# A block of windowed attention and mixed experts on one core: expert weights from another DMA queue, and another order in the tail

## What is computed

```
h = layernorm(x) * (1 + ca) + sa
x = x + ga * attention(h)
h = layernorm(x) * (1 + cb) + sb
x = x + gb * experts(h)

attention: q, k, v = h @ wq, wk, wv              16 heads of 8 channels
  local  = softmax over a causal window of 32, on k and v
  remote = softmax over 64 pooled latents (8 heads), then @ r_out_w
  out    = (sigmoid(q . gl) * local + sigmoid(q . gr) * remote) @ w_out

experts: g   = mean over tokens of (relu(h @ gate_w1.T + gate_b1) @ gate_w2.T + gate_b2)   one of 8 per expert and batch
  mW1 = W1 + sum over e of g[e] * TW1[e]         F = 512 rows of 128
  mW2 = W2 + sum over e of g[e] * TW2[e]         128 rows of 512
  out = gelu(h @ mW1.T + mb1) @ mW2.T + mb2      biases mixed likewise
```

## Time and profile before

| | us |
|---|---|
| three runs | 706.54, 707.58, 707.37; median 707.37 |
| profiled execution, its own time | 706.55 |
| its span in the trace | 704.7 |
| busy in the span: PE / PE weight loads / DVE / ACT / POOL | 662.0 / 503.2 / 542.8 / 382.1 / 217.1 |
| chain that ended last, shares | PE 78%, DVE 16%, issue 3%, ACT 1% |
| DMA: SP's queue (q1) / POOL's queue (q0) | 18.25 MB, 10.7% / 6.31 MB, 5.8% of the 16 engines |

### The profile page before, as it was taken

How to read it: one execution, slowest core, us unless ns; L and a number is a source line. 1 busy time by engine, 2 the same in 40 slices (tenths; PEclk the granted TensorE clock), 3 DMA queues, 4 the chain that set the end, 5 groups by cost and what they waited for, 6 DMA issues and landing times.

```text
span 704.7 us, 24615 instructions
## 1 busy us (share of the span) xinstructions
PE 662.0 (94%) x9075; PEld 503.2 (71%) x9075; DVE 542.8 (77%) x1242; ACT 382.1 (54%) x907; POOL 217.1 (31%) x351
## 2 busy tenths in 40 slices
PE   4698999999999999999999999999869999999998
PEld 2365676667766667776667666677559899998996
DVE  5777898999998999999999989998757255472552
ACT  2264666567766577765677665677522423324232
POOL 3344444344533345443345443454320000000000
PEclk9799999999999999999999999999979999999999
DMA  4656410110011110101100101100500110000001
GB/s 108 170 79 87 57 31 22 30 30 22 22 30 24 34 24 22 30 22 28 32 22 22 30 22 30 30 15 16 74 3 2 30 32 7 30 22 30 30 8 52
DMA packets 65797, 24.84 MB, mean 35 GB/s; under 512 B 38440, under 2 KB 64360, under 8 KB 65648
## 3 DMA queue, kind: packets, MB, share of 16 engines
q1 hardware_dynamic: 64320, 18.25, 10.7%
q0 software_dynamic: 1456, 6.31, 5.8%
HBM read 16.13 MB, written 8.40 MB: 35 GB/s over the span
## 4 chain that ended last, share of the span: by engine, by line
PE 78%; DVE 16%; issue 3%; ACT 1%; DMA 0%; POOL 0%; DVEq 0%; SPq 0%; POOLq 0%
PE SB L822 8%; PE WB L810 8%; PE SB L889 7%; DVE rden L639 7%; PE WB L975 7%; PE WB L921 5%; PE WB L940 5%; PE WB L797 4%; PE WB L925 4%; PE SB L797 4%; DVE mx L553 3%; DVE Pr L560 3%; PE SB L1036 3%; PE WB L849 3%; PE WB L837 3%
## 5 line engine op out<-in xcount | busy, mean ns | idle before, releaser
L390 ACT ACTIVATE Pr<-Pr 128x512 f32<-128x512 f32 x128 | 77.8, 638 | 130.8 <-DVE Pr L560 130.6
L498 ACT ACTIVATE Pr<-WB,mb1T 128x256 f32<-128x256 f32 x128 | 49.8, 477 | 75.7 <-PE WB L810 75.6
L560 DVE TENSOR_TENSOR Pr<-SB,mx 128x512 f32<-128x512 f32 x128 | 84.9, 684 | 3.6
L553 DVE TENSOR_REDUCE mx<-SB 128x8 f32<-128x512 f32 x128 | 84.6, 682 | 3.8 <-PE SB L874 3.8
L364 POOL TENSOR_TENSOR attT<-a_gated,rem_g 128x256 f32<-128x256 f32 x32 | 23.2, 724 | 172.7 <-DVE a_gated L654 172.7
L395 ACT COPY PT<-SB 128x512 f32<-128x512 f32 x128 | 75.1, 589 | 2.1 <-PE SB L889 2.1
L639 DVE RECIPROCAL rden<-WB 128x256 f32<-128x256 f32 x32 | 56.2, 1758 | 22.0 <-PE WB L925 22.0
L335 POOL TENSOR_TENSOR KM<-K_ch,bd_scale 128x1024 f32<-128x1024 f32 x32 | 60.6, 1894 | 37.9 <-ACT K_ch L407 37.9
L889 PE MATMUL SB<-ident,Pr 128*128 128x128 f32 x512 | 66.8, 273 | 1.1 <-ACT Pr L390 1.0
L975 PE MATMUL WB<-GKBD,GQT 128*128 128x512 f32 (+1 forms) x128 | 56.4, 524 | 7.0 <-DVE wait_carrier L740 4.9
L889 PEld LDWEIGHTS SB<-ident,Pr 128*128 128x128 f32 x512 | 58.8, 141 | 5.1 <-ACT Pr L390 1.4
(11 more groups left out here) (188 smaller groups left out, 1419.7 us busy)
## 6 DMA issues: line engine op xcount, KB each, us to landing
x_all<-in_L_attn_x SPq DMA_DIRECT2D x32, 128.0 KB, 2.1
v_rows<-V_rows SPq DMA_DIRECT2D x32, 128.0 KB, 1.8
VBD<-v_rows SPq DMA_DIRECT2D x128, 32.0 KB, 1.8
TW<-in_L_ffn_TW POOLq DMA_DIRECT2D x16, 256.0 KB, 10.0
GA<-ga_rows POOLq DMA_DIRECT2D x1, 2048.0 KB, 11.8
out_x<-attT SPq DMA_DIRECT2D x16, 128.0 KB, 1.8
out_x<-y_ga SPq DMA_DIRECT2D x16, 128.0 KB, 1.8
PT<-in_L_ffn_W SPq DMA_DIRECT2D x2, 256.0 KB
```

Of the source, the lines that this page charges most:

```text
L390: nc.scalar.activation(Pr[:, k, :], Pr[:, k, :], ACT.Exp).then_inc(p_ready, 1)
L553: nc.vector.tensor_reduce(mx[:, k, :], SB[k][:].rearrange("p (h j) -> p h j", h=8), AX.X, ALU.max).then_inc(mx_ready, 1)
L560: nc.vector.tensor_tensor(Pr[:, k, :].rearrange("p (w h c) -> p h w c", w=2, h=8), SB[k][:].rearrange("p (h w c) -> p h w c", w=2, h=8), b ...
```

## The change

Three things change. First, `load_experts` moves from POOL to SP: SP writes out its steps 3 to 10 and issues expert it - 3 at the end of each, behind VBD, so two DMAs of 256 KB a step; its loop covers 11 to 30. POOL's `after` keeps only the load of GA. Second, `experts(0, 1, 0)` moves on DVE and PE from behind step B + 1 to behind step B + 2; on PE it stands in front of the waits and mixes that were there. Third, DVE's steps B + 2 and on no longer put y_ga first: it stands at the usual place, in step B + 2 behind the statistics of batch 30.

```diff
@@ -278,13 +278,22 @@
                         sp.dma_start(VBD[W * h:W * h + W, :, h, :], v_dram[:, h, :].rearrange("(k c) n -> c k n", c=W)
                                      ).then_inc(vbd_loaded, 16)
 
+            def load_experts(e):
+                sp.dma_start(TW1[J * e:J * e + J], ins["L0_ffn_TW1"][e].rearrange("(i j) h -> j i h", j=J)
+                               ).then_inc(tw_loaded, 16)
+                sp.dma_start(TW2[J * e:J * e + J], ins["L0_ffn_TW2"][e].rearrange("(i j) f -> j i f", j=J)
+                               ).then_inc(tw_loaded, 16)
+
             step(0)
             sp.wait_ge(zeros_ready, 1)
             load(rest_w, w_loaded)
 
             step(1)
             step(2)
-            with sp.Fori(3, B - 1) as it:
+            for it in range(3, 3 + E):
+                step(it)
+                load_experts(it - 3)
+            with sp.Fori(3 + E, B - 1) as it:
                 step(it)
             step(B - 1)
             step(B)
@@ -313,12 +322,6 @@
             nc.gpsimd.affine_select(out=tri[:], in_=tri[:], compare_op=ALU.is_ge, fill=0.0, base=0,
                                     pattern=[[-1, P]], channel_multiplier=1).then_inc(mask_ready, 1)
             nc.gpsimd.memset(VBD[:], 0.0).then_inc(pv_done, 1)
-
-            def load_experts(e):
-                pool.dma_start(TW1[J * e:J * e + J], ins["L0_ffn_TW1"][e].rearrange("(i j) h -> j i h", j=J)
-                               ).then_inc(tw_loaded, 16)
-                pool.dma_start(TW2[J * e:J * e + J], ins["L0_ffn_TW2"][e].rearrange("(i j) f -> j i f", j=J)
-                               ).then_inc(tw_loaded, 16)
 
             def inv_std(b, aggr, mv, ve, eps, rstd, rstd_s):
 
@@ -372,9 +375,6 @@
                     pool.dma_start(ga_dram, ga_row).then_inc(ga_stored, 16)
                     pool.wait_ge(ga_stored, 16)
                     pool.dma_start(GA[:], bc(ga_dram.rearrange("b d -> (b d)"), [P, B * D], 0)).then_inc(ga_loaded, 16)
-                if 1 <= it < 4 or it == B:
-                    for e in range(2 * (it - 1), 2 * it) if it < 4 else range(6, E):
-                        load_experts(e)
 
             pipeline(pool, step, after)
 
@@ -585,9 +585,6 @@
                                         bc(GA[:, bass.ds(b * D, D)], [P, T, D], 1), ALU.mult).then_inc(yga_ready, 1)
 
             def step(it):
-                tail = isinstance(it, int) and it >= B + 2
-                if tail and has(it, 3):
-                    output_times_ga(it - 3)
                 if has(it, 4):
                     dve.wait_ge(x1_ready, it - 4 + 1)
                     stats(x_all[:, bass.ds((it - 4) * S, S)], st_d, stat_d, mv_d, aggr_d, it - 4)
@@ -613,7 +610,7 @@
                 if has(it, 1):
                     latent_lowered(it - 1, *latent_tiles[0])
                     latent_maximum(it - 1, 1, NL)
-                if has(it, 3) and not tail:
+                if has(it, 3):
                     output_times_ga(it - 3)
                 if has(it, 1):
                     latent_lowered(it - 1, *latent_tiles[1])
@@ -695,7 +692,7 @@
                 nc.vector.tensor_tensor(gmb2T[:, cols], mb2T[:, cols], gbT[:, cols], ALU.mult).then_inc(g_ready, 1)
 
             def after(it):
-                if it == B + 1:
+                if it == B + 2:
                     experts(0, 1, 0)
                 if it == B + 3:
                     for m in range(8):
@@ -1054,9 +1051,8 @@
                 mm(biases[:, FC * n_b:(FC + 1) * n_b], tb2[:], gT[:, cols], start=True, stop=True).then_inc(g_done, 1)
 
             def after(it):
-                if it == B + 1:
+                if it == B + 2:
                     experts(0, 1, 0)
-                if it == B + 2:
 
                     pe.wait_ge(tw_loaded, N_TW)
                     pe.wait_ge(g_ready, N_G0)
```

## The result

The changed kernel takes 703.76 us, the median of five runs (701.43 to 704.37), beside 707.37 us for the kernel before on the same chip. The ratio is 0.9945 with an interval of 0.9926 to 0.9964: 0.55% faster. The forecast was 703.2 us. The profiled execution took 703.73 us, its span is 701.8 us against 704.7 us.

The account below looks back on a forecast made before the run. It took PE's chain of waits as the bound, with 5.5 us lost in steps 3 and 4 beside POOL's loads. Front -5.5 plus tail +1.3 gave -4.2: 703.2 us from the median 707.37; range 701.2 to 706.8.

Parts of the forecast that it names:

- The front: Steps 3 and 4: waits, stops and low clock go, 2.09 + 2.14 + 1.32 = 5.55, taken as 5.5 us gained.
- Parts 1 and 2: Steps 3 and 4: PE's waits before the latent scores go (2.09 us), and stops inside the scores go (2.14 us).
- first rival: Stops inside the scores come from code length alone and stay, with the low clock; 706.6 us, chance 12%.
- part 2: Steps 3 and 4: instruction fetches no longer meet expert loads, so both stops inside the scores go, 2.14 us.
- Part 3: Step 3's gates (L951) through the next first projection run at full clock without the idle stretches: 1.32 us gained.
- SP's load: Two more DMAs on SP in each of eight steps fit into its 8.6 us gap and cost 0.
- room of 17.7 us: Time SP's added loads may take before costing: gap 8.6, wait for values 2.7, slack before V_rows copy 6.4 us.
- part 4: SP's added issues (0.9 us a step) and 512 KB transfers (some 5 us) fit its gap, costing 0.
- The tail: After the last attT: projection and statistics come earlier, but gates at low clock stand before the mixes; 1.3 us lost.
- from there the order is that of before: Tail after batch 31's transposes, forecast at 526.1 against 524.76: same order as before, so the loss stays 1.3 us.
- mild rival: The tail costs nothing: clock stays up or returns sooner, gates take 1.7 us; 701.9 us, chance 16%.

Follow-up runs that it names:

- loads alone: Kernel before with the expert loads moved to SP as in the change, tail as before; 701.99 us, ratio 0.9926.
- burst from SP: Kernel before with SP issuing the expert loads at POOL's old moments (behind steps 1, 2, 3 and 32), tail as before; 712.18 us, ratio 1.0068.
- POOL paced: Changed kernel's tail, but POOL issues the loads, one expert in each of steps 3 to 10, its steps 0 to 10 written out; 710.29 us, ratio 1.0043.
- 1 MB a step: Changed kernel with two more unused 256 KB loads behind each expert on SP; 706.05 us, ratio 0.9973.
- 2 MB a step: Changed kernel with six more unused 256 KB loads behind each expert on SP; 760.65 us, ratio 1.0748.
- tail-only: Kernel before with the tail of the change, loads still on POOL; 708.65 us, ratio 1.0013.
- order-only: Kernel before with only DVE's tail order changed, statistics of batch 30 ahead of the last y_ga; 706.84 us, ratio 0.9992.
- gates-only: Kernel before with only the first gates moved behind step B + 2; 711.15 us, ratio 1.0056.
- the fillers: Unused products in PE's idle time: changed kernel, one place, 702.44 us; kernel with gates taken apart and spread earlier, three places, 695.45 us.

## Why the prediction was right

**The front, 5.5 us forecast.** The loads alone bring 5.2 us by the ratio. In the pair of profiles it is 4.82, and 4.68 + 1.28 = 5.96 for steps 3 and 4 alone; what lies between is the long step 2, in which PE does the same work in both and the clock stays low for longer. Step 3 was forecast at 14.3 us and took 13.79, step 4 at 15.6 and took 15.68.

*Parts 1 and 2* came true in the result, but they are not two gains that stand side by side. The run with the burst on SP shows that the time of POOL's issues (1.68 us in step 3) was hidden behind the late fetch: with the issues gone and the burst left, the whole 3.35 us became one stop. Only the sum of 4.23 us could be had, and only by moving the burst. The first rival, which was to keep the stops and still win 2.09, was priced wrongly for the same reason, and so was the expectation of 705 us for that run. That the stops are the loads' doing is shown by this table, read from the DMA view in narrow stretches and from the timelines of PE. "Burst" is the time from the first packet of the expert loads to the last (or of the unused loads beside them), "fetch" the packets of q8.

| kernel, place | burst | fetch, us it took | PE goes on at | stopped for |
|---|---|---|---|---|
| before, step 3 | 50.0 to 60.4 | 59.95, 1.15 | 62.50 | 1.67 |
| before, step 4 | 67.5 to 77.0 | 76.84, 1.21 | 79.41 | 0.47 |
| burst from SP, step 3 | 50.6 to 59.9 | 61.17, 1.19 | 63.55 | 3.49 |
| burst from SP, step 4 | 68.2 to 77.6 | 78.40, 1.14 | 80.91 | 1.59 |
| burst from SP, tail | 501.4 to 511.0 | 510.27, 1.80 | 513.45 | 2.74 |
| POOL paced, step 3 | 54.3 to 59.2 | 58.29, 1.78 | 61.26 | 2.41 |
| POOL paced, step 4 | 72.0 to 76.3 | 75.64, 2.05 | 79.10 | 3.19 |
| 1 MB a step, step 4 | 60.6 to 69.4 | 69.37, 1.85 | 72.51 | 2.28 |
| 2 MB a step, step 4 | 59.5 to 78.4 | 78.65, 1.11 | 81.03 | 8.43 |
| changed, step 3 | none | 57.27, 0.96 | | 0 |
| changed, step 4 | 61.4 to 66.7 | 63.09, 1.91; 71.61, 0.88 | | 0 |
| loads alone, step 4 | 61.8 to 66.0 | 67.02, 1.20; 72.22, 1.29 | | 0 |

In all nine stops the fetch comes when the burst is nearly or just through, and PE goes on 1.2 to 1.4 us after the fetch has landed. The burst comes from either queue, with 0.5 to 2 MB, and the longest burst goes with the longest stop. Where a burst ended early in the step, PE did not stop, whether the step's first fetch came in it (changed) or just behind it (loads alone); the second one, which was late in the kernel before (76.84), then comes 5 us after the burst, as part 2 had it. The burst isn't the only thing that makes such a stop: the 1 MB kernel has one of 0.17 us in step 2, ahead of its first expert load, 1.4 us after a fetch that landed at 43.61. So a small part of a stop can be the code's own, as the first rival says.

The rule quoted in the prediction from the Trainium skill (DMA: Bandwidth & Descriptors, section Issuing engines are not separate DMA queues), that another issuer saves only the time of issuing, fits here: SP at POOL's moments brought no gain, but a loss of 4.8 us. What the change wins comes from the moment, not from the queue: expert 0 is issued at 60.3 us, after the fetch at 57.27.

*Part 3*, the clock: forecast 1.32 us for L951 and the projection behind it. In this pair of profiles they give 1.92 - 1.13 = 0.79 and 1.06 - 0.59 = 0.47 us, 1.26 in all. As a term of its own that was luck. In the tail-only, order-only and gates-only kernels, with the loads still on POOL and the stops of step 3 in place, the clock did not fall in step 3: the gates take 1.03 us there (in the gates-only kernel it fell in step 4 instead). Yet steps 3 and 4 together take 35.35, 35.08 and 36.26 us, against 35.43 in the kernel before, because PE then waits longer for GKBD in step 4, 1.66 to 1.67 us and not 0.41. So what the clock costs is for the most part time that PE would have waited anyway. The sum of 5.5 us is right, as what two steps lie above the steady one; how it splits into parts 1 and 3 changes from one profile to the next.

**SP's load, 0 forecast.** The verdict was right, the room of 17.7 us was not. That step of part 4 added up the slack in front of three waits, as for one late transfer. A load that comes back every step can't use slack twice: SP's own round has to fit into the step, so between the end of the VBD issue and the landing of the V_rows store there are 14.95 - 1.8 = 13.1 us. With 1 MB it takes 8.6 + 3.3 = 11.9 us, and the steps stay at 14.95 to 14.98 us. With 2 MB it takes 4.4 + 17.1 = 21.5 us, and the step becomes 23.3 us. By the 17.7 us that step should have cost 3.8 us, not 8.3.

**The tail, +1.3 us forecast.** By the ratios it is 0.9 us (tail alone), and 1.3 and 0.6 us (the two builds of the changed kernel against the loads alone); the intervals are about as wide as that. The forecast's path fits at nearly every link, counted from attT:

| | forecast | changed kernel |
|---|---|---|
| statistics of batch 30 | -0.1 | -0.16 |
| xn_d of batch 30 | 2.0 | 2.05 |
| its transposes | 3.0 | 2.99 |
| twelve small matmuls take | 3.0 | 2.73 |
| mixes | 10.1 | 9.82 |
| transposes of batch 31 | 13.2 | 13.37 |
| ffn1 against before | +1.3 | +1.96 |

The last line misses 0.7 us. The mixes begin 0.97 us late, and from them to `ffn1` it takes 10.28 us against 9.28: the first sixteen mix matmuls take 3.76 us against 3.20, the next sixteen 2.23 against 1.95. The clock comes back later in them than before, which "from there the order is that of before" left out. And the pair of profiles is not the whole case: with the very order of before, the loads-only kernel had its mixes at 9.65 and ffn1 at 19.77 us, only 0.3 us better than the change, since the clock fell 0.3 us into its small matmuls. Over all profiles `ffn1` comes 19.46 to 20.79 us behind attT with the new order (changed kernel twice, tail alone, POOL paced, 1 MB, 2 MB; 19.9 on average) and 18.14 to 19.77 us with the old one (before, loads alone, burst from SP; 19.1 on average). What the new order costs depends on when the clock falls, and the old order can pay nearly the same. That is why the times show less than 1.96 us, and that the forecast of 1.3 us fits is in part luck. The mild rival (clock up, tail free) needs idle times filled; the fillers show that the changed order doesn't get there by itself.

**Open.** How the chip orders a fetch among the packets of a burst isn't shown: the trace has no record of when PE asked, and in the 2 MB kernel one fetch came 1.7 us into the burst while the next had to wait for its end. A run in which POOL issues at exactly SP's moments wasn't made. The tail's cost is known to about 1 us only.

## What to carry to other kernels

A stop in the middle of like matmuls with "issue" as its cause, and packets of the instruction queue just before it ends, point to a PE that has run out of code; the DMA view tells whether a bulk transfer was in front of the fetch. Issue bulk loads behind the fetch that the first pass through a loop or a straight stretch needs, or in passes of a loop that is already there; which queue issued them mattered little here. For a transfer that repeats, the room is the step less the queue's own round, not the slack of all waits added up, and small dependent work ahead of a chain's last link belongs into idle time before it.

## What the runs showed of the hardware

- Expert loads into 16 partitions run at some 105 to 115 GB/s from either queue: four from POOL land in 9.0 us, and the 2 MB kernel moves 105 GB/s from 108 to 127 us, with the DMA engines nearly full (96% of the 16).
- An instruction fetch of 16 KB takes 0.96 us with nothing else under way (changed kernel, 57.27). In all nine stops it came only when a burst of 4.3 to 18.9 us was ending or over, yet one that came 1.7 us into a burst of 0.5 MB got through in 1.91 us. The stops of PE were 0.47 to 8.43 us long.
- Five and a half products that nobody reads, spread over three idle times, kept the granted clock of the tail at 1.00 where it was 0.50, and won 3.0 us between attT and `ffn1`, 2.6 us in the time. Five in one place did not.
